# The order of work set anew on TensorE, ScalarE, VectorE and GpSimd in a transformer block

## The chip, the cores and the metric

One core of one Trainium2 chip. The time is that of one execution on the device in microseconds; the kernel before was run three times. TensorE is written PE, VectorE DVE, ScalarE ACT, GpSimd POOL and SyncE, which issues most DMAs, SP in the rows of the profile.

## What is computed

x has 2048 tokens of 128 features. With modulation columns sa, ca, ga, sb, cb, gb made from a vector c:

```python
mod = (_silu(L0_c) @ L0_wmod).reshape(L0_c.shape[0], 6, 1, -1)
h = _layernorm(x, axis=-1) * (1 + ca) + sa
q = (h @ Wq + bq) / sqrt(dk);  k = h @ Wk + bk;  v = h @ Wv + bv
weights = softmax(where(causal, q @ k.T, -inf))
x = x + ga * ((weights @ v) @ Wo + bo)
h = _layernorm(x, axis=-1) * (1 + cb) + sb
prob = softmax(h @ w_router + b_router)          # 16 blocks of 32 channels, the best 4 are kept
y = (relu(h @ w1.T + b1) * mask_of_top_4_blocks) @ w2.T + b2
x = x + gb * y
```

## The kernel before

The tokens lie in four groups of 512 (g = 0 to 3), each of four tiles of 128. Matrix products are made to f32 precision from three products of rounded halves (hi and lo): `three` issues w_hi x m_hi, w_lo x m_hi, waits for the low half and issues w_hi x m_lo. Wq and Wk are folded into one matrix (fold), Wv, Wo and ga into another (back).

Each engine runs one long queue in the order of a plan written out by hand, `TENSOR_PLAN`, `SCALAR_PLAN`, `VECTOR_PLAN` and `GPSIMD_PLAN`. A word is a letter, the kind of step, and a number. `run` calls the step's function; semaphores hold it until its inputs are there, and all that stands behind a waiting step on its engine waits too. What the letters mean, by engine:

TensorE. i: a filler matmul of 256 columns on zeros, whose number means nothing (12 of them, behind 10 of 512 columns that are not in the plan). z: weight preparation (z0 the first two modulation columns, z1 and z2 the fold, z3 the other four columns, z4 and z5 back, z6 and z7 w1, z8 w2, z9 the router). n0 to n7: transposes of a group's normalised tokens, n0 to n3 for attention, n4 to n7 for the feed-forward layer. q: the folded query of a group. a0 to a39: scores of 128 queries against up to 512 keys, for the row maxima alone. b: transposes the maxima of a group, to be added to its query. s0 to s39: a tile of scores (128 keys by 512 queries, narrower on the diagonal). w0 to w39: weigh the values with tile t of the exponentials. o: output projection. r: router logits. m: transposes the chosen blocks. h and v: hidden units. d: the down projection. y: transposes the result.

VectorE. g: bn_stats and bn_aggr of a group (g0 to g3 of the input, g4 to g7 after attention). a0: normalises group 0. n, q: the low halves of transposed tokens and of the query. s0 to s39: the row maximum of the a tile of the same number. b: adds the maxima to row 0 of the query. i: masks a diagonal tile. x: divides by the softmax sum and adds to x. m, c: logits and the top 4. h, k: hidden units. f: the last addition. z6 adds the bias of w1, a row of 512 on one partition.

ScalarE. a1 to a7: normalise group 1 to 3 and, for the second layer, 0 to 3 (a4 to a7). n, q: high halves. e0 to e39: two exponentials of a score tile, p_hi and p_full; the second waits until the p_lo of two tiles before is made. c: copies the context. m, h, y: copies of choice, hidden and result.

GpSimd. z0: constants and the identity. z1, z7, z8: three masks, each a memset and an affine_select. z5: silu. z6: the gates. p0 to p7: (var + eps) to the power -0.5 and minus mean times that. u0 to u3: z_last, z_hi and z_lo of a group, the values' halves. l0 to l38: p_lo of a score tile. k0 to k11: hid_lo. z9, z10, z11: low halves of w1, w2 and the router.

Rules of the buffers: a, b, o and h share two turn banks in strict alternation in the order of `TENSOR_PLAN`, and each must wait until VectorE has read the bank two turns before; score tiles share three banks, each freed by the exponentials; TensorE's w_t needs e_t and l_t; d, r, o and m need what their names say. `apply(n)` on ScalarE needs p_n; p_n needs g_n; g4 to g7 need x0 to x3.

The input is loaded in groups by SP: x for group 0 in two halves first, then wk and two bias columns, then x for group 1 and 2, the second part of wmod, w1, w2, wv, wo, and x for group 3 late.

Of the kernel before, what the change touches and what calls it, by code (L numbers as in the profile page):

```python
# [38 lines left out]
UNDER = -87.33  # L39

TENSOR_PLAN = """
i0 i1 i2 z0 i3 i4 i5 i6 i7 z1 n0 i8 i9 z2 i10 i11 z6 z3 z8 q0 z9 n1 a0 z4 a1 a2 q1 a3 z5 a4 z7 a5 b0 a6 n2 a7
s0 a8 a9 s1 q2 a10 s2 a11 w0 a12 s3 b1 w1 a13 n3 a14 s4 a15 w2 a16 s5 a17 s6 a18 w3 a19 s7 s8 o0 w4 s9 w5 a20
a21 s10 q3 a22 w6 a23 w7 a24 w8 b2 s11 a25 w9 w10 a26 s12 a27 s13 a28 w11 a29 s14 a30 s15 a31 s16 w12 o1 w13
s17 s18 a32 a33 w14 s19 a34 a35 s20 w15 s21 a36 w16 a37 n4 a38 s22 s23 a39 w17 w18 w19 b3 w20 r0 w21 s24 w22
s25 w23 s26 s27 w24 m0 o2 s28 n5 s29 w25 w26 h0 s30 s31 r1 s32 h1 s33 w27 w28 w29 s34 m1 h2 s35 w30 n6 w31 s36
h3 h4 s37 r2 s38 w32 s39 w33 w34 w35 w36 h5 w37 w38 w39 d0 d1 o3 d2 m2 d3 h6 h7 d4 d5 y0 h8 h9 d6 n7 d7 h10 r3
d8 d9 y1 h11 m3 h12 h13 v12 v13 d10 d11 h14 v14 h15 v15 d12 y2 d13 d14 d15 d16 d17 d18 d19 y3 y4
"""
SCALAR_PLAN = """  # L50
z0 z1 n0 z3 z6 a1 q0 n1 z8 z4 q1 z5 a2 z9 z12 n2 e0 e1 q2 a3 e2 e3 e4 n3 e5 c0 e6 e7 e8 e9 q3 e10 e11 e12 e13
c1 e14 e15 e16 e17 e18 a4 e19 e20 e21 z7 n4 e22 e23 a5 e24 c2 e25 e26 m0 e27 e28 n5 e29 e30 h0 e31 a6 e32 e33
h1 m1 e34 e35 n6 h2 e36 e37 e38 e39 h3 c3 h4 h5 m2 y0 h6 h7 a7 h8 n7 h9 y1 h10 m3 h11 h12 h13 y2 h14 h15 y3 y4
"""
VECTOR_PLAN = """
g0 z1 a0 g1 n0 g2 z3 z10 z11 g3 q0 s0 n1 s1 s2 s3 q1 s4 z5 s5 b0 s6 s7 n2 s8 s9 s10 s11 s12 b1 s13 s14 s15 s16
s17 s18 s19 q2 n3 i8 x0 i9 s20 s21 i10 s22 s23 s24 b2 s25 i11 s26 s27 s28 s29 s30 s31 g4 q3 x1 z6 s32 s33 g5
s34 i20 s35 s36 i21 s37 s38 i22 i23 s39 n4 b3 m0 c0 x2 n5 g6 h0 m1 c1 h1 h2 n6 i36 h3 m2 i37 h4 i38 i39 c2 h5
x3 g7 h6 h7 h8 h9 n7 h10 m3 c3 f0 h11 f1 k12 k13 k14 k15 f2 f3 f4
"""  # L60
GPSIMD_PLAN = """
z0 z5 p0 z1 z7 p1 u0 z6 p2 z8 u1 p3 l0 l1 z4 l2 u2 l4 l5 l6 l7 l8 l9 l10 z11 u3 z10 l12 l13 l14 l15 l16 p4 l17
l18 l19 p5 l20 l21 l22 z9 l24 l25 l26 l27 l28 l29 p6 l30 l31 k0 l32 l33 k1 l34 k2 l35 l36 l37 l38 k3 k4 k5 p7
k6 k7 k8 k9 k10 k11
"""


# [1079 lines left out]
```

## Time and profile before

| what | value |
|---|---|
| time, three runs | 118.54, 118.75, 119.10 us; median 118.75 |
| span of the profiled execution | 117.1 us, first to last instruction |
| TensorE, matmuls | 110.9 us busy, 95% |
| TensorE, weight loads (beside matmuls) | 87.7 us, 75% |
| VectorE | 86.6 us, 74% |
| ScalarE | 75.4 us, 64% |
| GpSimd | 88.7 us, 76% |
| chain that ended last | TensorE 71%, GpSimd 13%, VectorE 6%, ScalarE 4%, issue 4% |

The profiled execution's own span is 117.1 us; the median of the runs is 1.65 us above it, which is the launch and end around the span. Times in the rows count from the start of the span. A timeline row has its start, its length, then engine, line, operation, what it writes and reads, and how many are merged; in square brackets stands the idle time of the engine before it and what ended it. A matmul's length holds its way through the array, so that it runs on over the start of the next one: the step from start to start is what it costs.

### The profile page before, as it was taken

The page shows a single profiled execution, that of the slowest core. Times are in us where ns is not written, and L with a number is a line of the kernel's source. Part 1 is how long each engine was busy: PE and PEld are TensorE (multiplying, and loading weights), DVE is VectorE, ACT ScalarE, POOL GpSimd, SP SyncE. Part 2 cuts the span into 40 slices and gives each one's busy share as a digit, 9 for nine tenths or more (in the row PEclk, how much of TensorE's full clock was granted, in tenths as well). Part 3 has the DMA queues.
Part 4 walks back from the last instruction along what each step waited for, and adds up shares of the span by engine and source line. Part 5 has one row for each costly group of instructions (what it writes and reads, how often), then busy time and mean ns, then how long its engine had stood idle before and what let it go on. Part 6 is the DMA issues. An engine that isn't in the chain of part 4 may idle for free.

```text
span 117.1 us, 1992 instructions
## 1 busy us (share of the span) xinstructions
PE 110.9 (95%) x583; PEld 87.7 (75%) x583; DVE 86.6 (74%) x312; ACT 75.4 (64%) x162; POOL 88.7 (76%) x122
## 2 busy tenths in 40 slices
PE   5998799999999999999999999999999999999980
PEld 1477675978888888878867987788889788865770
DVE  5669799998989989999888576825693945874521
ACT  2324968875984099559679959998075577536430
POOL 2566888999797989999896998999966798822000
PEclk9999999999999999999999999999999999999997
DMA  2796000000000000000000000000000000023033
GB/s 57 197 318 194 0 3 3 0 6 0 0 3 0 0 6 0 0 0 3 0 0 0 0 6 0 0 0 0 0 0 6 3 0 3 0 79 100 0 95 90
DMA packets 6290, 3.42 MB, mean 29 GB/s; under 512 B 1157, under 2 KB 5894, under 8 KB 6279
## 3 DMA queue, kind: packets, MB, share of 16 engines
q1 hardware_dynamic: 5846, 3.09, 9.2%
q10 hardware_dynamic: 432, 0.20, 0.6%
q8 instruction: 5, 0.08, 0.3%
q14 instruction: 7, 0.05, 0.2%
HBM read 2.24 MB, written 1.05 MB: 28 GB/s over the span
## 4 chain that ended last, share of the span: by engine, by line
PE 71%; POOL 13%; DVE 6%; ACT 4%; issue 4%; DVEq 0%
PE bank L848 17%; PE bank L852 17%; PE bank L849 16%; POOL p_lo L468 8%; PE bank L894 5%; PE bank L1116 4%; POOL rstd L393 3%; PE bank L965 2%; PE bank L875 2%; ACT xn L540 2%; PE bank L1053 2%; POOL neg_mean L391 1%; PE bank L1026 1%; ACT p_full L571 1%; DVE xn L649 1%
## 5 line engine op out<-in xcount | busy, mean ns | idle before, releaser
L468 POOL TENSOR_TENSOR p_lo<-p_full,p_hi 128x512 fp32r<-128x512 f32 (+2 forms) x36 | 42.4, 1202 | 3.9 <-ACT p_full L571 3.9
L564 ACT ACTIVATE p_hi<-bank 128x512 fp32r<-128x512 f32 (+2 forms) x36 | 20.7, 576 | 9.2 <-PE bank L852 4.6
L571 ACT ACTIVATE p_full<-bank 128x512 f32<-128x512 f32 (+2 forms) x36 | 20.6, 572 | 1.6 <-POOL p_lo L468 1.5
L474 POOL TENSOR_TENSOR hid_lo<-hid_full,hid_hi 128x512 fp32r<-128x512 f32 x12 | 15.8, 1321 | 3.9 <-ACT hid_hi L598 3.9
L675 DVE TENSOR_REDUCE cmax<-bank 128x1 f32<-128x512 f32 x24 | 16.1, 684 | 1.2 <-PE bank L894 1.0
L894 PE MATMUL bank<-zt_hi,g_hi 128*128 128x512 f32 (+3 forms) x40 | 15.6, 403 | 0.4 <-DVE g_hi L698 0.2
L848 PE MATMUL bank<-g_hi,zt_hi 128*128 128x512 f32 (+3 forms) x40 | 14.8, 370 | 0.0
L849 PE MATMUL bank<-g_hi,zt_lo 128*128 128x512 f32 (+3 forms) x40 | 14.6, 365 | 0.0
L852 PE MATMUL bank<-g_lo,zt_hi 128*128 128x512 f32 (+3 forms) x40 | 14.5, 363 | 0.0
L848 PE MATMUL bank<-p_hi,z_hi 128*128 128x512 f32 (+2 forms) x36 | 13.9, 385 | 0.0
L852 PE MATMUL bank<-p_lo,z_hi 128*128 128x512 f32 (+2 forms) x36 | 13.5, 376 | 0.1
L849 PE MATMUL bank<-p_hi,z_lo 128*128 128x512 f32 (+2 forms) x36 | 13.4, 373 | 0.0
L540 ACT ACTIVATE xn<-x,mean_rstd,rstd 128x127 f32<-128x127 f32 x28 | 11.5, 487 | 2.6 <-POOL mean_rstd L396 2.5
L771 DVE SCALAR_TENSOR_TENSOR hid_full<-bank,keep 128x512 f32<-128x512 f32 x12 | 8.2, 686 | 6.0 <-POOL hid_lo L474 4.2
L894 PEld LDWEIGHTS bank<-zt_hi,g_hi 128*128 128x128 f32 x40 | 7.4, 188 | 3.0 <-DVE cmax L675 0.4
L393 POOL TENSOR_TENSOR rstd<-rstd,pow_half 128x4 f32<-128x4 f32 x8 | 8.3, 1043 | 0.7
L598 ACT CAST hid_hi<-hid_full 128x512 fp32r<-128x512 f32 x12 | 7.5, 626 | 1.6 <-DVE hid_full L771 1.1
L848 PEld LDWEIGHTS bank<-g_hi,zt_hi 128*128 128x128 f32 x40 | 7.5, 189 | 1.2
L852 PEld LDWEIGHTS bank<-g_lo,zt_hi 128*128 128x128 f32 x40 | 7.5, 188 | 1.2
L849 PEld LDWEIGHTS bank<-g_hi,zt_lo 128*128 128x128 f32 x40 | 7.5, 189 | 1.1
L852 PEld LDWEIGHTS bank<-p_lo,z_hi 128*128 128x128 f32 x36 | 6.8, 188 | 1.7 <-POOL p_lo L468 0.6
L848 PE MATMUL bank<-hid_hi,w2t_hi 128*128 128x512 f32 (+1 forms) x20 | 7.7, 386 | 0.0
(190 smaller groups left out, 255.9 us busy)
## 6 DMA issues: line engine op xcount, KB each, us to landing
x<-in_L_attn_y_all_dram SPq DMA_DIRECT2D x3, 256.0 KB, 3.9
out_dram<-res SPq DMA_DIRECT2D x3, 256.0 KB, 2.3
w<-in_L_ffn_w_dram SPq DMA_DIRECT2D x2, 256.0 KB, 5.0
x<-in_L_attn_y_all_dram SPq DMA_DIRECT2D x2, 128.0 KB, 2.9
wmod<-in_L_wmod_dram SPq DMA_DIRECT2D x1, 256.0 KB, 4.4
out_dram<-res SPq DMA_DIRECT2D x2, 128.0 KB, 1.8
wmod<-in_L_wmod_dram ACTq DMA_DIRECT2D x1, 128.0 KB, 3.2
wk<-in_L_attn_Wk_dram SPq DMA_DIRECT2D x1, 64.0 KB, 3.0
```

The lines of the kernel that those rows point to most:

```text
L393: last = pool.tensor_tensor(rstd[:, k, t], rstd[:, k, t], pow_half[:], ALU.pow)
L468: pool.tensor_tensor(p_lo[:, s, w:], p_full[:, n % 2, w:], p_hi[:, s, w:].bitcast(F32), ALU.subtract).then_inc(p_lo_pool, 1)
L474: pool.tensor_tensor(hid_lo[:, m, :], hid_full[:, n % 2, :], hid_hi[:, m, :].bitcast(F32), ALU.subtract).then_inc(hid_lo_pool, 1)
L540: last = nc.scalar.activation(norm_rows(n)[:, i, 1:], x[:, t, 1:], ACT.Identity, bias=mean_rstd[:, k, t:t + 1], scale=rstd[:, k, t:t + 1])
L564: nc.scalar.activation(p_hi[:, s, w:], src, ACT.Exp).then_inc(p_hi_s, 1)
L571: nc.scalar.activation(p_full[:, n % 2, w:], src, ACT.Exp).then_inc(p_full_s, 1)
L675: nc.vector.tensor_reduce(cmax[:, n, c:c + 1], src, AX.X, ALU.max, negate=True).then_inc(turn_out, 1)
L771: nc.vector.scalar_tensor_tensor(out=hid_full[:, n % 2, :], in0=turned_bank(f"h{n}")[:], scalar=0.0, in1=grp(keep, g), op0=ALU.max, op1=AL ...
L848: mm(dst, w_hi, m_hi, start=start, stop=False)
L849: mm(dst, w_lo, m_hi, start=False, stop=False)
L852: return mm(dst, w_hi, m_lo, start=False, stop=stop)
L894: last = mm(dst[:, 0:w], tile(g_hi, g * GT + r), zt_hi[:, c * GW:c * GW + w], start=True, stop=not masked)
```

## The change

The four plans hold the same words in another order. No operation, no wait and no buffer is added or removed; but which bank a turn step gets, and which step frees it, follow from the order of a, b, o and h on TensorE. The lines moved:

```diff
 TENSOR_PLAN = """
-i0 i1 i2 z0 i3 i4 i5 i6 i7 z1 n0 i8 i9 z2 i10 i11 z6 z3 z8 q0 z9 n1 a0 z4 a1 a2 q1 a3 z5 a4 z7 a5 b0 a6 n2 a7
-s0 a8 a9 s1 q2 a10 s2 a11 w0 a12 s3 b1 w1 a13 n3 a14 s4 a15 w2 a16 s5 a17 s6 a18 w3 a19 s7 s8 o0 w4 s9 w5 a20
-a21 s10 q3 a22 w6 a23 w7 a24 w8 b2 s11 a25 w9 w10 a26 s12 a27 s13 a28 w11 a29 s14 a30 s15 a31 s16 w12 o1 w13
-s17 s18 a32 a33 w14 s19 a34 a35 s20 w15 s21 a36 w16 a37 n4 a38 s22 s23 a39 w17 w18 w19 b3 w20 r0 w21 s24 w22
-s25 w23 s26 s27 w24 m0 o2 s28 n5 s29 w25 w26 h0 s30 s31 r1 s32 h1 s33 w27 w28 w29 s34 m1 h2 s35 w30 n6 w31 s36
-h3 h4 s37 r2 s38 w32 s39 w33 w34 w35 w36 h5 w37 w38 w39 d0 d1 o3 d2 m2 d3 h6 h7 d4 d5 y0 h8 h9 d6 n7 d7 h10 r3
-d8 d9 y1 h11 m3 h12 h13 v12 v13 d10 d11 h14 v14 h15 v15 d12 y2 d13 d14 d15 d16 d17 d18 d19 y3 y4
+z0 i0 i9 i6 i7 i11 i2 z1 i5 i1 i8 i10 i3 i4 z2 n0 z3 z8 q0 z6 n1 a0 a1 z4 z9 a2 z5 q1 a3 z7 a4 b0 n2 a5 a6 s0 a7
+s1 a8 s2 a9 q2 a10 s3 a11 w0 a12 w1 b1 w2 w3 a13 n3 a14 s4 a15 a16 s5 s6 a17 a18 s7 w4 a19 a20 s8 s9 o0 s10 q3
+a21 s11 a22 w5 a23 w6 a24 w7 b2 w8 w9 w10 a25 s12 a26 s13 a27 s14 a28 w11 s15 a29 s16 a30 n4 a31 w12 a32 a33 w13
+s17 a34 a35 s18 s19 a36 w14 a37 s20 o1 s21 s22 w15 s23 w16 a38 w17 a39 w18 w19 b3 w20 w21 r0 w22 s24 s25 h0 s26
+h1 w23 m0 s27 s28 n5 w24 o2 w25 r1 s29 s30 s31 w26 s32 w27 m1 s33 w28 h2 s34 s35 w29 s36 h3 n6 w30 s37 w31 s38
+w32 s39 w33 w34 r2 w35 w36 w37 w38 h4 w39 d0 h5 d1 o3 m2 d2 d3 h6 h7 d4 d5 h8 h9 d6 n7 h10 d7 r3 y0 d8 h11 h12
+m3 y1 d9 v12 h13 v13 d10 d11 h14 v14 h15 v15 d12 y2 d13 d14 d15 d16 d17 d18 d19 y3 y4
 """
 SCALAR_PLAN = """
-z0 z1 n0 z3 z6 a1 q0 n1 z8 z4 q1 z5 a2 z9 z12 n2 e0 e1 q2 a3 e2 e3 e4 n3 e5 c0 e6 e7 e8 e9 q3 e10 e11 e12 e13
-c1 e14 e15 e16 e17 e18 a4 e19 e20 e21 z7 n4 e22 e23 a5 e24 c2 e25 e26 m0 e27 e28 n5 e29 e30 h0 e31 a6 e32 e33
-h1 m1 e34 e35 n6 h2 e36 e37 e38 e39 h3 c3 h4 h5 m2 y0 h6 h7 a7 h8 n7 h9 y1 h10 m3 h11 h12 h13 y2 h14 h15 y3 y4
+z0 z1 z3 n0 a1 q0 n1 z4 z5 z6 q1 a2 z12 n2 z8 e0 e1 z9 q2 e2 e3 a3 c0 n3 e4 e5 e6 e7 e8 q3 e9 e10 e11 e12 e13 a4
+c1 e14 e15 n4 e16 e17 e18 z7 e19 e20 e21 e22 e23 a5 e24 e25 e26 m0 c2 h0 n5 e27 e28 e29 h1 e30 e31 e32 m1 e33 a6
+e34 e35 n6 e36 e37 e38 h2 h3 e39 c3 h4 h5 m2 y0 h6 h7 a7 h8 n7 h9 y1 h10 m3 h11 h12 h13 y2 h14 h15 y3 y4
 """
 VECTOR_PLAN = """
-g0 z1 a0 g1 n0 g2 z3 z10 z11 g3 q0 s0 n1 s1 s2 s3 q1 s4 z5 s5 b0 s6 s7 n2 s8 s9 s10 s11 s12 b1 s13 s14 s15 s16
-s17 s18 s19 q2 n3 i8 x0 i9 s20 s21 i10 s22 s23 s24 b2 s25 i11 s26 s27 s28 s29 s30 s31 g4 q3 x1 z6 s32 s33 g5
-s34 i20 s35 s36 i21 s37 s38 i22 i23 s39 n4 b3 m0 c0 x2 n5 g6 h0 m1 c1 h1 h2 n6 i36 h3 m2 i37 h4 i38 i39 c2 h5
-x3 g7 h6 h7 h8 h9 n7 h10 m3 c3 f0 h11 f1 k12 k13 k14 k15 f2 f3 f4
+g0 z1 g1 a0 g2 z3 n0 z10 z11 g3 s0 q0 n1 s1 s2 s3 z5 s4 b0 q1 s5 s6 s7 n2 s8 s9 s10 s11 s12 b1 s13 s14 s15 s16
+q2 s17 s18 n3 s19 s20 i8 i9 x0 s21 s22 i10 i11 s23 s24 b2 g4 s25 s26 s27 z6 s28 s29 s30 s31 s32 s33 s34 s35 n4
+s36 s37 i20 x1 i21 g5 s38 i22 s39 q3 i23 b3 m0 c0 h0 h1 n5 x2 m1 c1 g6 h2 i36 n6 i37 h3 i38 m2 i39 c2 h4 h5 x3
+g7 h6 h7 h8 h9 n7 h10 m3 c3 f0 h11 k12 f1 k13 k14 k15 f2 f3 f4
 """
 GPSIMD_PLAN = """
-z0 z5 p0 z1 z7 p1 u0 z6 p2 z8 u1 p3 l0 l1 z4 l2 u2 l4 l5 l6 l7 l8 l9 l10 z11 u3 z10 l12 l13 l14 l15 l16 p4 l17
-l18 l19 p5 l20 l21 l22 z9 l24 l25 l26 l27 l28 l29 p6 l30 l31 k0 l32 l33 k1 l34 k2 l35 l36 l37 l38 k3 k4 k5 p7
-k6 k7 k8 k9 k10 k11
+z8 z1 z0 z5 p0 p1 u0 z6 p2 p3 z7 u1 l0 l1 l2 z11 z4 u2 l4 l5 l6 l7 l8 l9 l10 p4 z10 l12 l13 l14 l15 l16 l17 l18
+l19 l20 l21 p5 l22 z9 u3 l24 l25 l26 k0 l27 l28 l29 l30 l31 p6 l32 l33 l34 l35 k1 l36 l37 l38 k2 k3 k4 k5 p7 k6
+k7 k8 k9 k10 k11
 """
```

## Rows read from the trace of the kernel before

**Rows 1.** The page: the engines, and an issue of DMAs (KB, us to landing).

```profile
PE 110.9 (95%) x583; PEld 87.7 (75%) x583; DVE 86.6 (74%) x312; ACT 75.4 (64%) x162; POOL 88.7 (76%) x122
...
x<-in_L_attn_y_all_dram SPq DMA_DIRECT2D x3, 256.0 KB, 3.9
```

**Rows 2.** Busy us by stretch: from:to, length, engines, granted clock, DMA.

```profile
0.00:19.99 19.99, 17.46 (x92) 11.68 (x93) 15.81 (x71) 10.72 (x28) 13.19 (x39) 1.00 0.40 113
19.99:60.00 40.01, 39.65 (x207) 33.06 (x206) 36.24 (x110) 28.07 (x63) 36.56 (x48) 1.00 0.01 1
```

**Rows 3.** Timeline of GpSimd: five splits.

```profile
42.71 6.29 POOL L468 TENSOR_TENSOR p_lo<-p_full,p_hi 128x512 fp32r<-128x512 f32 x5 [0.38 <-ACT p_full L571]
```

**Rows 4.** The chain that ended last, in order of time: start, us, what.

```profile
7.23 1.02 DVE xn L649 x4
8.25 0.79 DVE st L632 x4
...
9.54 0.25 POOL neg_mean L391
...
11.53 1.66 ACT xn L540 x4
```

**Rows 5.** Timelines of TensorE, VectorE and SP's queue, the start.

```profile
5.48 0.85 PE L1112 MATMUL bank<-filler 128*128 128x256 bf16 x3
6.12 0.65 PE L1061 MATMUL bank<-silu,wmod 128*128 128x1 f32 x4
...
2.06 0.91 DVE L832 MEMSET nmax<- 128x1024 f32 x1 [0.16 <-issue]
...
6.81 0.35 DVE L797 SCALAR_TENSOR_TENSOR lift<-base,bank 128x127 f32<-128x127 f32 x1 [1.59 <-PE bank L1061]
...
11.13 0.26 DVE L802 SCALAR_TENSOR_TENSOR fold_lo<-bank,fold_hi 128x128 fp32r<-128x128 f32 x1
...
3.23 0.98 SPq L338 DMA_DIRECT2D x<-in_L_attn_y_all_dram  x2
```

**Rows 6.** Timeline of GpSimd: the last operation of p2.

```profile
17.44 0.20 POOL L396 TENSOR_TENSOR mean_rstd<-neg_mean,rstd 128x4 f32<-128x4 f32 x1
```

**Rows 7.** Timelines of TensorE and VectorE from b0 to a14.

```profile
18.15 0.66 PE L913 MATMUL bank<-ident,nmax 128*128 128x128 f32 x4
...
18.99 0.68 DVE L701 TENSOR_TENSOR g_hi<-bank,g_hi 1x512 fp32r<-1x512 f32 x1
...
25.23 1.17 DVE L698 TENSOR_TENSOR g_hi<-bank,g_hi 1x128 fp32r<-1x128 f32 x4
...
26.45 0.33 PE L894 MATMUL bank<-zt_hi,g_hi 128*128 128x128 f32 x1 [0.15 <-DVE g_hi L698]
```

**Rows 8.** Timeline of TensorE around a34, and around w20 and r0.

```profile
50.47 0.39 PE L852 MATMUL bank<-g_lo,zt_hi 128*128 128x512 f32 x1
50.70 0.92 PE L894 MATMUL bank<-zt_hi,g_hi 128*128 128x512 f32 x2
51.45 0.39 PE L848 MATMUL bank<-g_hi,zt_hi 128*128 128x512 f32 x1
...
58.55 0.40 PE L849 MATMUL bank<-p_hi,z_lo 128*128 128x512 f32 x1
59.07 0.49 PE L852 MATMUL bank<-p_lo,z_hi 128*128 128x512 f32 x1
59.41 0.39 PE L976 MATMUL bank<-h_hi,wr_halves 128*32 128x512 f32 x1
```

**Rows 9.** Timelines of VectorE and GpSimd: b2, w1 bias, choice, p4.

```profile
39.09 1.18 DVE L698 TENSOR_TENSOR g_hi<-bank,g_hi 1x128 fp32r<-1x128 f32 x4
...
48.57 1.36 DVE L814 TENSOR_TENSOR w_full<-w_full,b_row 1x512 f32<-1x512 f32 x1
...
63.38 0.63 DVE L762 TENSOR_SCALAR chosen<-marked 128x512 bf16<-128x512 f32 x1
...
49.09 0.95 POOL L391 TENSOR_SCALAR neg_mean<-mv 128x4 f32<-128x4 f32 x1
```

## The prediction

> **What bounds the kernel now.** I read the totals first, then stretches of time, then the chain that ended last, then each engine's timeline where the two orders differ. TensorE is busy 95% of the 117.1 us span, the others 64 to 76% [rows 1]. By stretches, it idles 2.5 us before 19.99 us and 0.4 us from there to 60 [rows 2]. So a new order can win in three ways only: start the dense part earlier, take out stalls that a "busy" digit hides (a matmul record runs on over the next one's start), or shorten the tail. The tail's order (from y2 on) is unchanged. GpSimd is the second bound: five p_lo splits of 512 columns take 6.29 us there, one behind the other [rows 3], so 1.26 each, for about 1.4 us of TensorE work (a score tile and a weighing), and GpSimd is busy 36.6 of 40 us between 20 and 60 [rows 2]. All sums are made against this execution's span; the median, 118.75 us, lies 1.65 us above it, and I subtract gains from the median unchanged. Work and waits are the same set of words, each once per engine, so nothing is saved in work: only positions count. Over 0.5% (0.6 us) is about what a measurement of this kernel can tell from no change.
>
> **Start: what sets it.** The chain before 13.3 us runs: apply group 0 on VectorE (7.23), statistics of group 1 (8.25), GpSimd's power (9.54 to 11.5), apply on ScalarE (11.53), which TensorE's n1 awaits [rows 4]. The change edits this chain in three places.
> z0 on TensorE moves ahead of fillers i0 to i2: they start at 5.48, z0 at 6.12 now, so it is 0.64 earlier, and VectorE, which sits 1.59 us idle for it, builds lift1 at 6.17 instead of 6.81 [rows 5].
> VectorE's g1 moves ahead of a0. It no longer waits for the apply (7.2 to 8.25) [rows 4], but for its data: issued at 3.23, and landing 3.9 us after issue by the median row, 7.1 [rows 1, 5]. Statistics start at 7.2 instead of 8.2, 1.0 earlier. The price: group 0 is applied 8.3 to 9.4, 1.1 later, and zt_lo of group 0 ends near 11.4. That is hidden: q0 can't start before fold_lo, which ends at 11.39 today, behind g2 [rows 5], and stands ahead of zt_lo in the new order. Without that cover it would cost 1.1.
> GpSimd's z8 and z1 move ahead of z0, so the identity is ready at 2.9 instead of 1.6. VectorE asks for it at 2.97, after its nmax memset (2.06 for 0.91) [rows 5]: nothing, or 1.25 at most if the cover were gone.
> So p1 starts at 8.5 and a1 at 10.5, each 1.0 earlier. On GpSimd u0, z6 and p2 follow p1 back to back, and end at 17.64 [rows 6], 6.1 us behind p1; a1's lead passes on to p2, to a2 (17.7 becomes 16.7) and to n2 on TensorE. The order p2 p3, with z8 gone from between, brings p3 forward and u1 back by 1.2; l0 still starts about 1 us earlier.
> b0 on TensorE is held today to 18.15 [rows 7] by row maximum s4, whose bank a5, standing between, must have free; ahead of a5 it runs at about 16.9. The first scores come near 19.15 instead of 19.99.
>
> **Where the start's gain goes.** VectorE now has q1 and s5 (0.60 and 0.47 by their steps in the timeline) behind b0, which stood before it. Its chain from b0 to b1 took 18.99 to 25.23 [rows 7], 6.24 us with 0.3 idle. In the new order it is 5.9 + 1.1 = 7.0 us of work from 17.9, so b1 starts at 24.9 to 25.2: 0.0 to 0.3 of the 1.0 is left. But w2 and w3 (0.4 us of TensorE work) are done by then, ahead of a13 and n3. a14, which waits for b1 now (26.45, idle 0.15) [rows 7], comes 0.25 earlier with 0.4 more done. I take 0.6 as TensorE's lead (ends: 0 and 1.0).
>
> **Stalls that go.** At 50.70 two row-maximum matmuls hold 0.75 us until 51.45, where two cost 0.46: 0.29, for VectorE's banks behind x1, the w1 bias and s32, s33. At 59.07 w20's third matmul follows its second by 0.52 instead of 0.23 and the next record 0.34 later: 0.40, for l20, which stands on GpSimd behind p5 [rows 8]. In the change x1 and g5 stand behind i20, p5 behind l21, u3 (2.2 us) behind z9: l20 has 4.1 us less ahead of it. Both go: 0.69. Late next is VectorE's s31 (below).
>
> **Stalls that may come.** (1) Layer 2's first normalisation is pulled forward: g4 to just behind b2, p4 ahead of z10 and l12, a4 ahead of c1 and e14, n4 behind a30. Queued behind p4 on GpSimd are z10 and l12, for which w12 waits; behind n4 on TensorE is everything. b2 ends at 40.27 now [rows 9]; with the lead it ends near 39.2, if VectorE, which idles 3.8 us between 20 and 60 [rows 2], fills some 0.5 of that beside the lead. Then g4 (1.2) to 40.5, p4 (1.95) to 42.5, a4 (1.65) to 44.2, where TensorE arrives at 44.2 to 44.4: nothing. GpSimd stands empty from 38 to 40.5, then z10 and l12 end at 45.0, w12 needs it at 45.3: nothing, by 0.3 us. VectorE carries g4 and the w1 bias (1.36) ahead of s28, so a30 waits some 0.15. (2) From r0's start to m0 there are now 4.3 us of TensorE work (r0 0.45, five steps of three 512-column matmuls at 0.23 [rows 8] 3.45, w22 and w23 0.4); the choice took from r0's start, 59.41, to 64.01 on VectorE (63.38 for 0.63) [rows 8, 9]: 4.6 us. It costs 0.35 (0 to 0.6, if b3 is late on VectorE). (3) m1 has 4.65 us behind r1 and needs 4.4: 0. h3 on VectorE waits for k1, which moved behind l35; h5 and o3, that wait for it, come 4 us later: 0. The tail swaps (y0, y1, d7, h11, h12) change the order of the same work with h and d tiles as cover: 0, between -0.2 and 0.2.
>
> One place where a rule bears. p4's first operation took 0.95 us in the middle, against 0.25 for p1's [rows 4]; it began at 49.09 while VectorE added the w1 bias, two tensors in SBUF, from 48.57 to 49.93 [rows 9]. The Trainium skill, SBUF — State Buffer, on the shared port pair, says that VectorE with two SBUF inputs and a GpSimd operation that reads SBUF lock each other out, whoever starts first, for the whole instruction; the trace agrees. In the new order the bias add stands at about 42 to 43.4, against p4's end, z10 or l12. By the rule one of them waits up to 0.9 us and w12 up to 0.6: 118.5 instead of the sum below.
>
> **Sum.** 0.6 + 0.69 - 0.15 - 0.35 = 0.8 us: 118.75 - 0.8 = 117.95 us.
>
> **Rivals.**
> A, the start's gain ends on VectorE. The row maxima give b1 and b2 at their old times, so the lead is 0: 0.69 - 0.5 = 0.2, 118.55 us. For it: VectorE is busy 36.2 of 40 us there [rows 2]; against it: w2 and w3 are done early whatever b1 does.
> B, slower: the pulled-forward normalisation. With no lead b2 ends at 40.27, g4 at 41.5, p4 as it was before (2.6, with 0.95 for its first operation) at 44.1, a4 at 45.8; TensorE reaches n4 at about 45.1 and stands 0.7. z10 and l12 end at 46.6, and if the bias add holds one of them (0.9) at 47.5, where w12 wants it at 46.8: 0.7 more. With 0.15 and 0.35, less 0.69: 1.2 slower, 119.95 us. It decides from the point where b2 ends later than about 39.5; each 0.1 from there costs TensorE 0.1.
> C, no new stall and the whole lead: 1.0 + 0.69 = 1.7, 117.05 us.
> D, the clock. It is granted in full in both stretches [rows 2]. The new order leaves TensorE nearly empty from about 8.5 to 9.5 and again near 12. Were it granted half until 16, some 3 us of matmuls would take twice as long and 2 of it would reach the end: 121. Against it: today it idles 2.5 us in that stretch [rows 2] with no fall.
>
> **How the numbers follow.** The forecast has 0.45 (117.4 to 118.4; 0.40 of it is faster by over 0.5%, 0.04 within, 0.01 slower, its start or m0 worse than their bounds), C 0.10, A 0.24 (within 0.5%), B 0.13, D 0.03; 0.05 is for a joint that I followed wrongly, slower. Faster: 0.40 + 0.10 = 0.50. Same: 0.24 + 0.04 = 0.28. Slower: 0.13 + 0.03 + 0.05 + 0.01 = 0.22. The likeliest time is the forecast's. The range runs from just under C to just under B: 116.9 to 119.8.
>
> **What would show it.** The profile of the changed kernel should have x statistics of group 1 at 7.2, the first ScalarE apply at 10.5, n2 near 18.4 and the first scores near 19.2; b1's four row additions at 25.0 and b2's near 38; no 0.5 us step inside w20; r0 to m0 over 4.6 us. Wrong would be: b2 at 39.1 or later (A), GpSimd waiting for mv past 41 and ScalarE's a4 after 44.5 with TensorE idle ahead of n4 (B), matmuls of 512 columns at over 0.4 us apart after 8 us (D).

## The result and the profile after

The changed kernel takes 119.69 us (median of 13 runs, 119.54 to 121.5); the kernel before, run beside it, 118.83 (13 runs). The ratio is 1.0086, interval 1.0058 to 1.0113: slower by 0.9 us, where 0.8 less was forecast. The profiled execution took 119.62 us, with a span of 117.8. The runs of either kernel lie up to 2 us apart, which the experiments come back to; ratios leave out runs over 1.5% above the fastest of their kernel.

The page of the changed kernel, and its busy time by stretch (from:to, length, engines with busy us, granted clock, DMA), beside [rows 1, 2]:

```profile
span 117.8 us, 1992 instructions
...
PE 111.2 (94%) x583; PEld 88.2 (75%) x583; DVE 88.0 (75%) x312; ACT 76.3 (65%) x162; POOL 88.9 (75%) x122
...
0.00:19.99 19.99, 17.85 (x97) 12.94 (x98) 16.80 (x71) 10.65 (x28) 14.29 (x43) 1.00 0.40 113
19.99:60.00 40.01, 39.58 (x209) 33.18 (x209) 36.30 (x113) 29.70 (x66) 35.12 (x42) 1.00 0.01 1
60.00:90.00 30.00, 29.29 (x148) 23.46 (x146) 19.40 (x83) 21.99 (x46) 27.66 (x27) 1.00 0.00 1
90.00:117.80 27.80, 24.48 (x133) 18.61 (x132) 15.45 (x48) 13.92 (x24) 11.83 (x12) 0.97 0.13 39
```

The same rows of the kernel before, for the stretches that stood in no row yet:

```profile
60.00:90.00 30.00, 30.00 (x156) 24.77 (x155) 19.62 (x86) 23.07 (x49) 27.07 (x25) 1.00 0.00 1
90.00:117.80 27.80, 23.81 (x133) 18.16 (x131) 14.94 (x47) 13.52 (x24) 11.87 (x12) 0.96 0.14 39
```

Before 19.99 TensorE is busy 0.4 us more than it was, and has issued 97 matmuls by then where it had issued 92. From 60 to 90 it stands 0.7 us, where it stood not at all, and issues 148 where it issued 156. The gain was made, and lost behind 60 us.

To see where, I added up TensorE's lost time. Every step of the plan has a length where nothing holds it (0.69 us for three matmuls of 512 columns, 0.52 for 384, 0.89 for o, 0.45 for r, 0.24 for m, and so on, one list for all kernels). What the step takes to the next step's start, less that length, is counted as lost. The two profiles, in us:

| stretch of TensorE's plan | before | after | difference |
|---|---|---|---|
| to s0, the first scores | 4.99 | 4.01 | -0.98 |
| s0 to r0 | 2.30 | 2.05 | -0.25 |
| r0 to m0, the first choice | 0.19 | 1.04 | +0.85 |
| m0 to m1 | 0.09 | 0.08 | 0.0 |
| m1 to m2 | 0.36 | 1.17 | +0.81 |
| m2 to y2, and the end | 2.27 | 2.58 | +0.31 |
| sum | 10.20 | 10.93 | +0.73 |

The spans differ by 0.7. So the first 60 us win 1.23, and three places behind them give back 1.97.

**r0 to m0.** Timelines of VectorE, GpSimd and TensorE of the changed kernel (start us, length, engine, line, operation, what it writes and reads; in brackets the engine's idle time before it):

```profile
59.36 1.26 DVE L735 STREAM_TRANSPOSE swung_sums<-bank 32x128 f32<-32x128 f32 x4 [0.35 <-PE bank L977]
...
62.68 1.29 DVE L762 TENSOR_SCALAR chosen<-marked 128x512 bf16<-128x512 f32 x1
...
61.17 1.29 POOL L403 TENSOR_TENSOR z_lo<-xn,z_hi 128x512 fp32r<-128x512 f32 x1
62.41 3.95 POOL L468 TENSOR_TENSOR p_lo<-p_full,p_hi 128x512 fp32r<-128x512 f32 x3
...
64.03 0.40 PE L1001 MATMUL bank<-ident_b,chosen 128*128 128x128 bf16 x4 [0.67 <-DVE chosen L762]
```

VectorE's last operation of the choice, `chosen`, takes 1.29 us where it took 0.63 [rows 9], and TensorE's m0 waits for it. GpSimd's p_lo for l24, the first of the three in its row, began at 62.41, 0.27 before it, and takes 1.28 us: it ends at 63.69, and `chosen` 0.28 later, at 63.97.

**m1 to m2.** The same pair at group 2's choice, first of before, then of after:

```profile
87.30 0.91 DVE L762 TENSOR_SCALAR chosen<-marked 128x512 bf16<-128x512 f32 x1
...
86.21 1.72 POOL L468 TENSOR_TENSOR p_lo<-p_full,p_hi 128x384 fp32r<-128x384 f32 x2 [1.00 <-ACT p_full L571]
```

```profile
88.32 1.23 DVE L762 TENSOR_SCALAR chosen<-marked 128x512 bf16<-128x512 f32 x1
89.47 1.28 DVE L771 SCALAR_TENSOR_TENSOR hid_full<-bank,keep 128x512 f32<-128x512 f32 x2
...
86.72 2.55 POOL L474 TENSOR_TENSOR hid_lo<-hid_full,hid_hi 128x512 fp32r<-128x512 f32 x2
...
90.29 1.22 PE L965 MATMUL bank<-back,ctx_sb 128*128 128x129 f32 x8
```

GpSimd ends at 87.93 and at 89.27, `chosen` at 88.21 and at 89.55: 0.28 later both times. Behind it stand h4 and h5 on VectorE, whose banks TensorE's o3 needs (90.29, where 90.07 was possible, and its later matmuls are late too); from d1 to m2 TensorE loses 0.40, where it lost 0.02. The rest is lost at n6 and between n6 and d1. At n6 TensorE stands for a6 on ScalarE, a6 for p6 on GpSimd, which the new plan has behind l31; n6 follows 0.45 behind a matmul whose own step is 0.23:

```profile
78.59 0.40 PE L852 MATMUL bank<-h_lo,w1t_hi 128*128 128x512 f32 x1
79.04 0.66 PE L875 MATMUL bank<-ident,xn 128*128 128x128 f32 x4
...
75.36 0.23 POOL L391 TENSOR_SCALAR neg_mean<-mv 128x4 f32<-128x4 f32 x1
...
77.34 1.65 ACT L540 ACTIVATE xn<-x,mean_rstd,rstd 128x127 f32<-128x127 f32 x4 [1.22 <-POOL mean_rstd L396]
```

### The profile page after: what moved, and what is told of

Same layout as the page of the kernel before. It is cut to its first block, busy times and chain, and to the rows that moved or that the text cites. A ratio compares the mean times of both kernels' runs of the same rounds, so it can differ in the third digit from the quotient of the medians.

```text
span 117.8 us, 1992 instructions
## 1 busy us (share of the span) xinstructions
PE 111.2 (94%) x583; PEld 88.2 (75%) x583; DVE 88.0 (75%) x312; ACT 76.3 (65%) x162; POOL 88.9 (75%) x122
## 3 DMA queue, kind: packets, MB, share of 16 engines
HBM read 2.24 MB, written 1.05 MB: 28 GB/s over the span
## 4 chain that ended last, share of the span: by engine, by line
PE 73%; POOL 10%; ACT 6%; DVE 5%; issue 3%; DVEq 0%
PE bank L848 17%; PE bank L852 16%; PE bank L849 16%; PE bank L894 6%; PE bank L1116 4%; ACT xn L540 4%; PE bank L965 3%; PE bank L875 3%; POOL rstd L393 3%; POOL p_lo L468 2%; PE bank L1053 2%; DVE chosen L762 1%; POOL z_lo L403 1%; PE bank L1026 1%; DVE swung_sums L735 1%
## 5 line engine op out<-in xcount | busy, mean ns | idle before, releaser
L474 POOL TENSOR_TENSOR hid_lo<-hid_full,hid_hi 128x512 fp32r<-128x512 f32 x12 | 15.3, 1290 | 4.6 <-ACT hid_hi L598 4.6
L894 PE MATMUL bank<-zt_hi,g_hi 128*128 128x512 f32 (+3 forms) x40 | 14.9, 398 | 0.5 <-DVE nmax L678 0.4
L540 ACT ACTIVATE xn<-x,mean_rstd,rstd 128x127 f32<-128x127 f32 x28 | 11.6, 497 | 2.2 <-POOL mean_rstd L396 1.9
```

The source lines that it names most:

```text
L474: pool.tensor_tensor(hid_lo[:, m, :], hid_full[:, n % 2, :], hid_hi[:, m, :].bitcast(F32), ALU.subtract).then_inc(hid_lo_pool, 1)
L540: last = nc.scalar.activation(norm_rows(n)[:, i, 1:], x[:, t, 1:], ACT.Identity, bias=mean_rstd[:, k, t:t + 1], scale=rstd[:, k, t:t + 1])
L894: last = mm(dst[:, 0:w], tile(g_hi, g * GT + r), zt_hi[:, c * GW:c * GW + w], start=True, stop=not masked)
```

## The experiments

Every kernel was timed in 6 or 12 runs. "Lost" is the sum of the table above, by stretch. The plans are cut in three: the start and first half (TensorE to w20, ScalarE to a5, VectorE to c0, GpSimd to l22 and u3), the middle (TensorE to d3, VectorE to x3), and the tail.

**1. Which part of the order costs.** Four mixtures. The first has the new first part with the old rest.

```diff
-b3 w20 w21 r0 w22 s24 s25 h0 s26 h1 w23 m0 s27 s28 n5
+b3 w20 r0 w21 s24 w22 s25 w23 s26 s27 w24 m0 o2 s28 n5
...
```

> New order in all four plans up to w20, c0, a5 and u3, the old order behind. Theory T (TensorE's steps add up: the new order leads by 1.2 us at r0, loses 1.6 between r0 and d3, 0.3 in the tail): 118.8 - 1.2 = 117.6 us, 117.4 to 118.0. Rival R (the second half of the kernel is bound by something that the lead doesn't move, the choice or GpSimd): 118.6 to 118.9.

Measured: 119.03 us, ratio 1.0007 (0.9972 to 1.0042), over a microsecond above what theory T gave and just above the rival's range. The second has new first part and middle, old tail.

```diff
-d4 d5 h8 h9 d6 n7 h10 d7 r3 y0 d8 h11 h12 m3 y1 d9 v12 h13 v13 d10
+d4 d5 y0 h8 h9 d6 n7 d7 h10 r3 d8 d9 y1 h11 m3 h12 h13 v12 v13 d10
```

> New order up to d3 (k5, x3, h5 on the other engines), the old tail. T: the new tail costs 0.3, so 119.7 - 0.3 = 119.4 us. R: as the change, 119.7.

Measured: 119.35, 1.0075 (1.0041 to 1.0108). The third is the kernel before with the new tail alone, the same lines the other way round.

> Old order up to d3, new tail alone. T: 118.8 + 0.3 = 119.1 us. R: 118.8, nothing.

Measured: 119.09, 1.0040 (1.0015 to 1.0065). The fourth is the kernel before with the new middle alone.

```diff
-b3 w20 r0 w21 s24 w22 s25 w23 s26 s27 w24 m0 o2 s28 n5
+b3 w20 w21 r0 w22 s24 s25 h0 s26 h1 w23 m0 s27 s28 n5
...
```

> Old order up to w20 (c0, a5, z9 and u3) and from h6 on, the new middle alone. T: 118.8 + 1.6 = 120.4 us; less where GpSimd idles ahead of l24 in the old first part and so lets the choice through: 119.8 to 120.4. R: 119.5 to 119.7, since the middle's order sets the end whatever comes first.

Measured: 119.97, 1.0105 (1.0067 to 1.0144). What follows: the tail costs some 0.4 us wherever it stands (0.34 between the second mixture and the changed kernel, and 2.25 us lost from m2 to y2 against 1.87 before). The middle costs most, 1.2 us by itself: without the new start it loses 0.39 more than before from s0 to r0, 0.03 at m0 and 0.78 from m1 to m2. So the loss at m0 needs both parts. The first part with the old rest comes out even: its profile has lost 1.34 us from r0 to m0, for another reason. u3 now stands right ahead of l24, and TensorE waits for l24, not for the choice:

```profile
62.76 1.30 POOL L403 TENSOR_TENSOR z_lo<-xn,z_hi 128x512 fp32r<-128x512 f32 x1
64.02 2.76 POOL L468 TENSOR_TENSOR p_lo<-p_full,p_hi 128x512 fp32r<-128x512 f32 x2
...
65.60 0.51 PE L852 MATMUL bank<-p_lo,z_hi 128*128 128x512 f32 x1 [0.75 <-POOL p_lo L468]
```

**2. Is it GpSimd that holds `chosen`?** The operand `marked` goes to a PSUM bank, at first for group 0 alone, then for groups 0 to 2, in the changed kernel.

```diff
-    last = nc.vector.match_replace(marked[:, i, :], top8[:, i, :], keys[:, i, :], FURTHEST)
+    last = nc.vector.match_replace(marks[:, i, :], top8[:, i, :], keys[:, i, :], FURTHEST)
```

> The changed kernel, with the marks of group 0's choice kept in PSUM (free columns of norm_bank), so that the operation that makes `chosen` reads PSUM and not two ways from SBUF. Theory L (in the change it stood 1.29 us because a GpSimd split was running, until that ended): it takes 0.6 to 0.7 us whatever GpSimd does, m0 waits 0.3 instead of 0.9 us. End: 119.7 - 0.6 = 119.1 us if the lead is kept, 119.6 if it is given back at n6, which waits for GpSimd's p6. Rival (the operation is slow for another reason, its broadcast input): it stays at 1.2 to 1.3, and the time at 119.7.

> The same for groups 0, 1 and 2. L: `chosen` of group 2 falls from 1.23 to 0.65 too, c2, h4 and h5 end 0.5 earlier and o3 no longer waits 0.5: 119.7 - 0.6 - 0.5 = 118.6 us, 118.6 to 119.2. Rival (o3 waits for k2 and k3 on GpSimd, not for the choice): as with group 0 alone.

Measured: 119.59, 1.0088 (1.0061 to 1.0115), and 119.15, 1.0057 (1.0021 to 1.0094). In the first, from the view of the tile `chosen` (min, median and max in ns, first and last start):

```profile
L765 DVE TENSOR_SCALAR chosen<-marked x2: 426/875/1324, 72.7 to 89.0; 128x512 bf16<-128x512 f32 x2
L765 DVE TENSOR_SCALAR chosen<-bank x1: 691/691/691, 63.3 to 63.3; 128x512 bf16<-128x512 f32 x1
```

From PSUM it takes 691 ns beside a running GpSimd; from SBUF 426 where GpSimd's operation ends 0.13 us into it, or 1324 where that ends 1.04 us into it. The other profiles agree: 22 choices from PSUM took 0.69 us each, and the 23 from SBUF that lasted longer than 0.43 all ended 0.28 to 0.29 us behind a GpSimd operation that was running when they began. That settles the mechanism. r0 to m0 then loses 0.45 instead of 1.04. But with group 0 alone in PSUM nothing is won: m0 to m1 loses 1.14 where it lost 0.08, since group 1's choice now meets a p_lo. With all three it loses 0.52.

**3. m0 moved behind s27**, to give the choice time.

```diff
-h1 w23 m0 s27 s28 n5
+h1 w23 s27 m0 s28 n5
```

> The changed kernel with one word moved: m0 on TensorE behind s27 instead of ahead of it, 0.7 us of work between r0 and m0 more. Step 2 of the sum (too little work between r0 and m0) right: the stall at m0 falls from 0.9 to 0.2 and the end to 119.0 if the lead is kept; 119.6 if it is given back at n6 or o3.

Measured: 119.9, 1.0131 (1.0089 to 1.0173), above both times expected. r0 to m0 loses 0.34, but m0 to m1 1.38. The next kernel joins this with the old tail and the PSUM form:

> All together: the change up to d3, the old tail, m0 behind s27, marks in PSUM for groups 0 to 2. If the three losses (m0 0.9, o3 0.5, tail 0.3) are separate: 119.7 - 1.6 = 118.1 us, under the kernel before. If GpSimd's queue is the bound beneath them: 118.6 to 118.9.

Measured: 119.9, 1.0063 (1.0029 to 1.0098); r0 to m0 0.23, m0 to m1 0.90. So the stall had only moved: the two lose 1.13 together, as in the changed kernel (1.12). The median says less here, since in 7 of the 12 runs the clock fell for a while (experiment 8); the other five took 118.46 to 119.30.

**4. Control**: the kernel before with groups 0 to 2 in PSUM.

> Control: the kernel before with the marks of groups 0 to 2 in PSUM. Its choices took 0.63, 0.43 and 0.91 us; now each takes 0.69. As the stall between r0 and m0 is only 0.19 us there and no lead is to be lost, all theories expect 118.6 to 118.9, within 0.3% of the kernel before. If it came out slower by 0.4% or more, the form in PSUM has a price of its own (its keys are written and read more slowly), and what the changed kernel won by it would be understated.

Measured: 118.81, 1.0013 (0.9996 to 1.0030). The form has no price that these runs can tell.

**5. u3 back ahead of p4.** GpSimd stands empty there in the changed kernel:

```profile
35.67 1.79 POOL L468 TENSOR_TENSOR p_lo<-p_full,p_hi 128x384 fp32r<-128x384 f32 x2 [0.62 <-ACT p_full L571]
40.10 0.23 POOL L391 TENSOR_SCALAR neg_mean<-mv 128x4 f32<-128x4 f32 x1 [2.63 <-DVE mv L635]
```

```diff
-l8 l9 l10 p4 z10 l12
+l8 l9 l10 u3 p4 z10 l12
...
-p5 l22 z9 u3 l24
+p5 l22 z9 l24
```

> The changed kernel with GpSimd's u3 (2.2 us) back ahead of p4, in the 2.6 us that GpSimd stands empty there in the changed kernel. Theory (TensorE's lead of 1.2 us is lost because GpSimd, which works without a pause from p4 to k3, has no lead: l24 ends at 63.4 and k3 at 89.0 in both kernels): l12's end stays at 45.0, l24's end comes 2.2 us earlier, 61.2, p6, k1 and k3 up to 2 us earlier; the stalls at n6 (0.22) and d1/o3 (0.5) go, and the median is 118.9 to 119.3. The stall between r0 and m0 stays near 0.9 us, since the choice for group 0 still meets some running operation of GpSimd. Rival (GpSimd's place in the queue is not what costs; only the collisions of the choice with it do): the time stays at 119.5 to 119.8, with GpSimd merely idle more often after 62 us.

Measured: 119.06, 1.0031 (0.9995 to 1.0066), so 0.6 us better, the time that was expected, but from another place. I had expected the stall between r0 and m0 to stay and those at n6 and o3 to go. The reverse is seen: r0 to m0 loses 0.22 instead of 1.04, m1 to m2 1.16 as ever. l24 is no longer kept by u3; it starts when ScalarE has its input, overlaps `chosen` by 0.2 us alone, and the choice is on time:

```profile
64.67 0.47 DVE L762 TENSOR_SCALAR chosen<-marked 128x512 bf16<-128x512 f32 x1
...
63.56 3.96 POOL L468 TENSOR_TENSOR p_lo<-p_full,p_hi 128x512 fp32r<-128x512 f32 x3 [1.34 <-ACT p_full L571]
...
65.19 0.40 PE L1001 MATMUL bank<-ident_b,chosen 128*128 128x128 bf16 x4
```

**6. The sum of the remedies.** First u3 ahead of p4 with the old tail; then the same with group 2's choice in PSUM.

> The new order up to d3 and the old tail behind it, with u3 ahead of p4: the run with u3 alone (119.06) and the old tail, which won 0.3 us in the kernel that differs from the changed one in it alone. If the two causes are separate, 118.6 to 118.9 (ratio to the kernel before 0.999 to 1.002), with no stall at m0 over 0.3 us, none at m1, and 0.4 to 0.5 us still lost from d1 to m2, where the choice of group 2 meets a running operation of GpSimd. Rival: the tail's loss exists only where GpSimd is late, and the time stays at 119.0 to 119.1.

> As the run before this one, with group 2's marks in PSUM. Theory: the loss from d1 to m2 is the choice of group 2 held by GpSimd's k2 (1.23 us where it takes 0.69 in the form that doesn't wait): that loss falls from 0.45 to under 0.1, and the time is 118.2 to 118.5, under the kernel before by 0.2 to 0.4%. Rival (m2's loss has another cause, the place of h4 and h5 behind the choice): it stays, and the time is 118.6 to 118.9.

Measured: 118.78, 1.0006 (0.9973 to 1.0038), and 118.44, 0.9974 (0.9943 to 1.0005). The tail gives 0.3 again, and group 2's choice 0.3 more: from d1 to m2 there are 0.01 us lost, where the run without it lost 0.40. `chosen` runs through beside GpSimd:

```profile
87.88 0.69 DVE L765 TENSOR_SCALAR chosen<-bank 128x512 bf16<-128x512 f32 x1
...
86.25 2.56 POOL L475 TENSOR_TENSOR hid_lo<-hid_full,hid_hi 128x512 fp32r<-128x512 f32 x2
```

**7. Where m0 stands.** All remedies at once, with m0 late and six fillers moved, and then the same with m0 back ahead of s27.

> All remedies together: the new order up to d3, the old tail behind it, m0 behind s27, the marks of groups 0 to 2 in PSUM (so that no choice waits for GpSimd), u3 ahead of p4, and six fillers behind z2. If the four causes are what they seem (fall of the clock, choice behind a running operation of GpSimd, GpSimd without a lead, the new tail), their shares add up: from 119.7, less 0.3 for the tail, 0.5 for m0, 0.5 for u3, 0.2 for the fillers: 118.2, under the kernel before (118.7 to 118.8) by 0.5 us. The rival: TensorE's lead is again taken back between s28 and m1, as in the run with all groups of marks in PSUM, by VectorE: 118.9 to 119.2, and m1 stands 0.5 us or more.

> As the kernel with all remedies (118.77), but with m0 back ahead of s27. There 0.94 us were lost between s28 and m1. Theory: m0's later place is the cause (m0 on TensorE, ScalarE's copy of it, VectorE's h0 and h1, which the new order puts ahead of n5, x2 and group 1's choice: 9.6 us from one choice to the next, where the changed kernel took 8.9). Then r0 to m0 loses 0.2 us more and s28 to m1 0.6 less: 118.3 to 118.5, and 8.9 to 9.3 us from choice to choice. Rival (the form in PSUM is the cause, 0.27 us more for each of the two choices, wherever m0 stands): s28 to m1 still loses over 0.7 us and the time is 118.8 to 119.0.

Measured: 118.77, 1.0009 (0.9993 to 1.0026), and 118.38, 0.9958 (0.9925 to 0.9991). The second is the one kernel of this study that beats the kernel before beyond its interval. From r0 to m0 it loses 0.45 against 0.23, from m0 to m1 0.25 against 0.91. The new order has h0 and h1 ahead of n5, x2 and group 1's logits on VectorE, and they await m0 by way of ScalarE: a later m0 makes the next choice later. From the end of one `chosen` to the end of the next the kernel with m0 late takes 9.57 us (63.65 to 73.22), the other 9.15 (64.45 to 73.60).

**8. The start.** Six of the twelve fillers behind z2, in the changed kernel, and three of them in the kernel with u3, the old tail and group 2 in PSUM.

```diff
-z1 i5 i1 i8 i10 i3 i4 z2 n0
+z1 z2 i5 i1 i8 i10 i3 i4 n0
```

> The changed kernel with six of its twelve filler matmuls (i5 i1 i8 i10 i3 i4) behind z2 instead of ahead of it, so that they fill what TensorE leaves empty ahead of n0 (0.8 to 1.0 us in the three profiles of the new start in which the granted clock fell to half near 11 us; nothing in the others). Theory (the new start itself risks the fall: idle TensorE between z2 and n0, since group 0 is applied behind g1): no fall in this profile whatever the time at which the clock rose, the largest idle stretch of TensorE between 6 and 10 us at most 0.4 us, the timed runs closer together, and a median 0.1 to 0.4 us under the changed kernel's, so 119.2 to 119.5. Rival (the fall comes from something else, or the fillers are too small to matter): a fall at about 11 us whenever the clock rose before 5 us, and the median stays at 119.6 to 119.8. A rival on the other side: z2's place ahead of the fillers moves nothing, but n0 is now behind six fillers where the clock is still half then, 0.2 us each: 0.3 to 0.5 us later at n1, 120.0.

> As the run with u3 ahead of p4, the old tail and group 2's marks in PSUM, with three of the fillers (i10 i3 i4) behind z2. With six behind it a profile whose clock rose late lost 0.4 us ahead of n1, but none of 12 runs was over 119.2 us in the kernel with all remedies. Theory: three of them lose at most 0.1 us and still cover part of the empty stretch: 118.2 to 118.5 with fewer runs over 119.5 than the kernel without (3 of 12 expected there). Rival: the fillers' place changes neither.

Measured: 119.86, 1.0112 (1.0075 to 1.0148), and 118.46, 0.9987 (0.9949 to 1.0025), from 117.98 to 119.9. Neither is faster than the same kernel without the edit, and the spread stays. One cause is in VectorE's timeline. The kernels with u3 ahead of p4 and the old tail, with group 2 in PSUM and without, have the same start; their profiled executions took 118.5 and 119.98 us, and the second had lost 1.19 us more by n1. No fall of the clock is in either. What differs is this, in that order:

```profile
7.08 0.87 DVE L633 BATCH_NORM_STATS2 st<-x 128x6 f32<-128x128 f32 x4 [0.28 <-DMA x<-in_L_attn_y_all_dram]
```

```profile
8.28 0.87 DVE L632 BATCH_NORM_STATS2 st<-x 128x6 f32<-128x128 f32 x4 [1.51 <-DMA x<-in_L_attn_y_all_dram]
```

Over the fourteen profiles with g1 ahead of a0 the statistics of group 1 start between 6.72 and 8.28 us, in twelve of them when the rows land. TensorE's n1 follows: in the ten of them without a fall of the clock it starts 5.2 to 5.5 us later, from 12.05 to 13.47. Group 0's apply stands behind the statistics, so that a late landing delays both groups. In the kernel before, a0 covers the landing, and g1 starts at 8.17 in the timeline (8.25 in the chain of [rows 4]). The last two runs put a0 back ahead of g1, in the kernel of 118.38 and in that of 118.44.

```diff
-g0 z1 g1 a0 g2 z3 n0
+g0 z1 a0 g1 g2 z3 n0
```

> The fastest kernel so far (new order with u3 ahead of p4, old tail, all three choices in PSUM, six fillers behind z2; 118.38, 118.02 to 119.25) with VectorE's a0 back ahead of g1, where the kernel before has it. What this tells apart: in the ten profiles of the new start, group 1's statistics began between 6.7 and 8.3 us, held by the landing of group 1's rows in all but one, and group 0's apply stands behind them; with a0 first it can't be late. Theory (the late runs of the new start are those in which the rows land late): a0 at 6.8 to 7.2, n1 with 2.1 to 2.6 us of TensorE's time lost ahead of it in any run, the highest timed run under 119.0, the lowest 118.2, since the early start of g1 (up to 1.1 us) is given up; median 118.3 to 118.6. Rival (the spread is the clock's alone): the highest stays at 119.2 or more, and the median rises by 0.5 us or more, the lead being gone.

> The same edit (VectorE's a0 ahead of g1) in the kernel with u3 ahead of p4, the old tail and group 2's choice in PSUM, which has the fillers where the changed kernel has them (118.44, 117.77 to 119.64, 4 of 12 over 119). Theory of the late rows: at most 1 of 12 over 119, lowest 118.1 to 118.3, median 118.3 to 118.5. Rival (clock, or g1's lead is what wins): 3 or more of 12 over 119, or a median over 118.7.

Measured: 119.01 (118.95 to 119.5), 1.0022 (0.9994 to 1.0050), and 119.22 (118.95 to 119.61), 1.0034 (1.0007 to 1.0060). The spread shrinks from 1.23 to 0.55 us and from 1.87 to 0.66, but only because the fast runs are gone: the lowest is 118.95 both times, where 118.2 was expected, and the highest stay (119.5 after 119.25, 119.61 after 119.64). By the conditions set beforehand both results are the rival's: the highest run stayed above 119.2 and the median rose by over 0.5 us in the first, and in the second 10 of 12 runs are over 119. In the six profiles with a0 first the statistics start at 7.82 to 8.19 and n1 5.05 us later. So a0 first makes every run nearly as late as the late landings did. The early g1 is worth 0.63 and 0.78 us in the median and 0.9 to 1.2 in the lowest run, and makes no run slower that these series show.

The clock is the second source. In five of the sixteen profiles that have the new plan of TensorE up to w20 (four of the fourteen, and the last kernel) the granted clock reached full speed between 4.15 and 4.77 us and fell to half between 11.0 and 11.6. Stretches of the kernel with u3 alone:

```profile
8.00:11.30 3.30, 2.07 (x16) 1.62 (x16) 3.23 (x21) 0.90 (x3) 1.93 (x5) 1.00 0.99 316
11.30:14.70 3.40, 3.40 (x15) 3.00 (x15) 3.33 (x13) 2.19 (x5) 2.88 (x7) 0.50 0.02 4
```

and from its timeline, TensorE's n0:

```profile
9.42 1.00 PE L875 MATMUL bank<-ident,xn 128*128 128x128 f32 x4 [1.23 <-DVE xn L649]
```

In the 3.3 us ahead of the fall TensorE was busy for 2.07, and idle for 1.23 in one piece, waiting for group 0's apply; then came 3.4 us at half clock (1.2 of 2.4 GHz). These profiles have lost 2.9 to 4.0 us by the end of n1, against 1.7 to 3.2 in the others. None of the four profiles with the old start has a fall there, but in none of them did the clock rise before 5.6 us; and with six fillers behind z2 and a rise at 4.85 there was none either.

The timed runs tell more. The mean granted clock of a whole execution is 0.984 to 0.986 in the five profiles with the fall and 0.994 to 1.00 in the other fifteen, and every timed run is either at 0.979 to 0.986 or at 0.993 or more. Counting those below 0.99 as runs with a fall:

| kernels | runs with a fall |
|---|---|
| the kernel before, beside the eighteen experiments | 22 of 139 |
| new TensorE plan up to w20, fillers where the change has them (11 kernels) | 30 of 121 |
| three fillers behind z2 | 4 of 12 |
| six fillers behind z2 (4 kernels) | 0 of 42 |

So the fall is not the new order's alone: the kernel before has it in one run of six, and then takes 120.07 us (median) where it otherwise takes 118.62. And it does not make the 0.9 us that the change costs: 2 of the changed kernel's 13 runs have it, and without these the median is 119.62. Six fillers behind z2 go with its absence. What in TensorE's work they alter, a shorter idle stretch or another, is not shown: a profile with six of them still idles 0.85 us in one piece.

## Why the prediction was wrong

**The start: right, and a little better than forecast.** First scores came at 18.89 (19.15 forecast), statistics of group 1 at 6.72 (7.2), b1's additions at 24.78 (25.0), b2's at 37.64 (38). TensorE's lead was 0.98 us at s0 and 0.85 by a14; I took 0.6. The last two runs give a size for g1's place by itself, 0.63 and 0.78 us. What the step missed is that "lands at 7.1" is a value of one execution: it ranges over 1.5 us, and the old order hid that. Rival A, with the lead ending on VectorE, is out: b2 stands 1.45 us earlier.

**The stalls that go: right.** In w20 the matmuls now follow at 0.24 and 0.23 where a step of 0.52 stood, and a34 and a35 hold 0.39 us (47.74 to 48.13) instead of 0.75 (compare [rows 8]):

```profile
57.40 0.47 PE L848 MATMUL bank<-p_hi,z_hi 128*128 128x512 f32 x1
57.70 0.40 PE L849 MATMUL bank<-p_hi,z_lo 128*128 128x512 f32 x1
57.94 0.39 PE L852 MATMUL bank<-p_lo,z_hi 128*128 128x512 f32 x1
58.17 0.34 PE L848 MATMUL bank<-p_hi,z_hi 128*128 128x384 f32 x1
```

Together that is 0.76 us, where 0.69 was forecast. The forecast gave two 512-column steps, 0.46, as what a34 and a35 cost; a35 has 384 columns.

**The pulled-forward normalisation: missed by 0.6 us.** The forecast had nothing here, and rival B 0.7 us. TensorE waited for xn:

```profile
43.77 0.40 PE L894 MATMUL bank<-zt_hi,g_hi 128*128 128x512 f32 x1
44.59 0.66 PE L875 MATMUL bank<-ident,xn 128*128 128x128 f32 x4 [0.41 <-ACT xn L540]
```

The step took 0.82 us where 0.23 is usual, so 0.59 were lost. g4's result was there at 40.1, as worked out, but p4 took 2.75 us instead of 1.95, since its last operation took 1.01 us where p5's took 0.20:

```profile
41.84 1.01 POOL L396 TENSOR_TENSOR mean_rstd<-neg_mean,rstd 128x4 f32<-128x4 f32 x1
...
58.14 0.20 POOL L396 TENSOR_TENSOR mean_rstd<-neg_mean,rstd 128x4 f32<-128x4 f32 x1
...
41.71 1.06 DVE L814 TENSOR_TENSOR w_full<-w_full,b_row 1x512 f32<-1x512 f32 x1
```

It began inside VectorE's bias add and ended 0.08 us behind it. The prediction had named this very meeting, with up to 0.6 us at w12, and left it out of the sum; the price came at n4. The first 60 us still won 1.23, where the forecast's terms make 1.14, and that is partly luck: the lead was 0.98 where 0.6 was put down, and the stalls that went gave 0.76 for 0.69, which nearly pays for the 0.59 at n4 that stood in no term.

**r0 to m0: the step that failed.** "It costs 0.35": the choice was taken to last the 4.6 us that it lasted before [rows 8, 9]. It lasted 5.28 us from r0's start (58.69 to 63.97), 0.66 of the 0.68 more in its last operation, which is held until GpSimd's running one ends; the place of l24 relative to it had changed. m0 lost 0.85 us more than before. The row that I had used showed 0.63, which was itself held (p_lo ended at 63.73, 0.28 before it); the same operation took 0.43 and 0.91 us for groups 1 and 2 of that execution. A duration that differs between three equal operations was the sign, and I had read it as a constant. The Trainium skill, SBUF — State Buffer, section "Who interferes with whom", says of VectorE in a two-port mode and GpSimd that whoever issues first has the shared port pair for the whole instruction while the other blocks. The Trainium skill, VectorE: DVE Perf Modes, section "Why PSUM operands drop a tier", says that the two-port mode needs both SBUF read ports, so that an operand in PSUM rules it out. The traces agree with both: held from SBUF it ends 0.28 to 0.29 us behind GpSimd's operation each time, from PSUM it takes 0.69 us always.

**The second half: two omitted terms.** I priced everything behind m1 at 0. It cost 0.81 from m1 to m2. Of this about 0.4 is the same hold at group 2's choice, which the run with that choice in PSUM shows; for the rest p6's later place is read from the waits at n6 alone, and no run moved p6 alone. The tail cost 0.31, above my bound of 0.2. In the tail TensorE goes into v12, h13, v13 where v12 and v13 stood together, and the step from the last matmul of a product to v, and from v to the next, is 0.32 where 0.23 is usual. With two such passages more, I estimate that 0.2 of the 0.3 us come from there; it was not tried by itself.

```profile
104.64 0.39 PE L852 MATMUL bank<-hid_lo,w2t_hi 128*128 128x512 f32 x1
104.96 0.38 PE L1026 MATMUL bank<-shut,spread 16*128 16x512 bf16 x1
105.28 0.50 PE L848 MATMUL bank<-h_hi,w1t_hi 128*128 128x512 f32 x1
```

**Account.** Forecast: +0.6 +0.69 -0.15 -0.35 = 0.8 us faster. Measured in the profiles: +1.23 to r0, -0.85 to m0, -0.81 to m2, -0.31 behind it = 0.73 slower. With u3 moved, choices in PSUM and the old tail the time came to 118.38 to 118.44, 0.3 to 0.5 us under the kernel before, less than half of the 1.23. From r0 to m2 the best two kernels still lose 1.05 to 1.11 us, against 0.64 before.

**The rivals.** B had the right sign and nearly the size (119.95), which is luck in the main: its stall ahead of n4 came (0.59 for 0.7), by p4's held last operation and not for want of a lead, but the rest of its price did not, and the time was lost behind 60 us. D happened as a mechanism, in some executions only, and in the kernel before as well. The one that came true, a choice on VectorE caught by GpSimd, was not among them, though the prediction named the very rule for p4.

**Open.** Why the kernel with only group 2 in PSUM still loses 0.79 us from m1 to d1, where the one with all three loses 0.39 (but 0.25 ahead of m1, where the other loses 0.04); what fixes the moment at which the clock rises, and by what the fillers keep it from falling.

## What to carry to other kernels

Before reordering, list for each engine pair that can hold one another the durations of equal operations: where they differ by more than a few per cent, the operation is not a cost but a meeting, and a shift of 0.5 us on one engine reprices it. A lead on the busiest engine is worth only what the next queue can match: count where the helper engine stands empty in the new order (2.63 us here) before counting the gain. And judge a step that is moved to wait for a load over many runs, by its median and both ends: here it won 0.6 to 0.8 us in the median, while the runs of one kernel differ by 1.2 us and more.

## What the runs showed of the hardware

- An SBUF-to-SBUF `chosen` of 512 columns on VectorE takes 0.43 us, or until 0.28 to 0.29 us behind the end of the GpSimd operation that runs when it begins, whichever is later: 0.63, 0.91, 1.23, 1.29, 1.32 us. From PSUM it takes 0.69, beside a running GpSimd operation or not.
- The hold goes both ways: an operation of 128 x 4 on GpSimd took 1.01 us instead of 0.20 beside a VectorE addition of two tensors in SBUF on a single partition, and ended 0.08 us behind it.
- The granted clock reached full speed between 4.15 and 7.2 us in executions of nearly the same instructions. In four of them it rose before 4.5 us, TensorE then idled 0.8 to 1.2 us in one piece between 8.1 and 9.4, and it fell to half for 3.4 us near 11.2. With six filler matmuls moved behind z2 no fall was seen in 42 runs, with the fillers ahead of it in 30 of 121.
